# Head attention from one product, and sums, shifted copies and the router moved into other stages

## The reference

```python
x = x + L0_attn_a(ln(x))   # head attention (16 heads of 8, no mask) + state-space scan + gated MLP
x = x + L0_ffn(ln(x))      # two layers: window attention, gated MLP, both on token-shifted input
x = x + L0_attn_b(ln(x))   # head attention, causal
x = x + L0_ffn(ln(x))
x = x + L1_attn_a(ln(x))   # head attention, causal, rotary, with biases
x = x + L1_ffn(ln(x))      # router, top 2 of 8 experts, layer norm of the sum
x = x + L1_attn_b(ln(x))   # random-feature attention
x = x + L1_ffn(ln(x))
```

## Time and profile before

| | |
|---|---|
| median of the runs | 6315.28 us |
| the profiled execution | 6308.24 us |
| its span, first to last instruction | 6306.2 us |
| busy: TensorE, VectorE, ScalarE, GpSimd | 5418.4, 3589.7, 3331.1, 2512.4 us |
| mean granted TensorE clock | 0.948 |

### The profile page before, as it was taken

One profiled execution on the slowest core, in us unless ns is written; L12 is line 12 of the kernel. 1 busy time (PEld: TensorE's weight loads), 2 busy tenths in 40 slices (PEclk: granted clock), 3 DMA queues, 4 the chain that ended last, 5 costly groups with the idle time before them and its releaser, 6 DMA issues. The chain is left out here.

```text
span 6306.2 us, 119595 instructions
## 1 busy us (share of the span) xinstructions
PE 5418.4 (86%) x42357; PEld 2908.8 (46%) x42357; DVE 3589.7 (57%) x4103; ACT 3331.1 (53%) x4993; POOL 2512.4 (40%) x1721
## 2 busy tenths in 40 slices
PE   6876888888887998998898998999897999776998
PEld 2432555555544553564344554554343444343443
DVE  4557999999954554554344554554454343554344
ACT  4555888888854553554444554454343333443343
POOL 1223999999933651652122661662221000000000
PEclk8996999999998999999899999999899999998999
DMA  1002111101011110110000110110000210001121
GB/s 41 1 0 77 31 32 30 33 30 33 29 47 29 40 40 14 41 41 13 1 0 18 45 40 12 42 40 20 28 0 8 54 40 13 0 0 27 32 36 27
DMA packets 136966, 171.03 MB, mean 27 GB/s; under 512 B 32352, under 2 KB 85728, under 8 KB 135520
## 3 DMA queue, kind: packets, MB, share of 16 engines
q1 hardware_dynamic: 136800, 168.85, 10.2%
HBM read 80.11 MB, written 12.85 MB: 15 GB/s over the span
## 5 line engine op out<-in xcount | busy, mean ns | idle before, releaser
L2318 POOL TENSOR_TENSOR arena<-arena,wbig 128x1024 f32<-128x1024 f32 x512 | 1191.8, 2515 | 103.5 <-DMA wbig<-scratch_b 100.3
L2305 DVE TENSOR_TENSOR_SCAN arena<-banks,arena 128x1024 f32<-128x1024 f32 x512 | 1141.5, 2279 | 63.7 <-ACT banks L2249 45.5
L944 ACT ACTIVATE arena<-banks,wbig 128x512 f32<-128x512 f32 x512 | 352.0, 688 | 584.3 <-PE banks L907 572.7
L601 DVE TENSOR_REDUCE arena<-banks 128x4 f32<-128x1024 f32 (+1 forms) x384 | 401.9, 1047 | 432.8 <-PE banks L435 305.1
L957 DVE TENSOR_TENSOR arena<-arena 128x512 f32<-128x512 f32 x512 | 353.3, 692 | 490.2 <-ACT arena L944 434.7
L768 POOL TENSOR_TENSOR X<-X,Z 128x1536 f32<-128x1536 f32 x2 | 9.5, 4758 | 1482.6 <-ACTq L761 1482.6
L1462 POOL TENSOR_TENSOR arena<-arena 128x512 f32<-128x512 f32 x256 | 355.5, 1389 | 594.5 <-DMA arena<-arena 594.5
L2249 ACT ACTIVATE banks<-banks 128x1020 f32<-128x1020 f32 x512 | 518.2, 1012 | 104.3 <-PE banks L2170 96.8
L2254 ACT COPY arena<-banks 128x1024 f32<-128x1024 f32 x512 | 520.8, 1017 | 51.4 <-POOL arena L2318 30.8
L547 ACT ACTIVATE Y<-banks 128x2048 f32<-128x2048 f32 x192 | 305.8, 1593 | 408.4 <-PE banks L471 311.4
L907 PE MATMUL banks<-Z,wbig 128*128 x1024 | 462.2, 597 | 34.3 <-ACTq L56 34.3
(11 more groups left out here) (289 smaller groups left out, 10428.3 us busy)
## 6 DMA issues: line engine op xcount, KB each, us to landing
arena<-arena SPq DMA_DIRECT2D x1024, 64.0 KB, 2.0
arena<-scratch_g SPq DMA_DIRECT2D x32, 1024.0 KB, 13.8
wbig<-scratch_d SPq DMA_DIRECT2D x512, 16.0 KB, 1.7
wbig<-scratch_b SPq DMA_DIRECT2D x64, 128.0 KB, 2.2
wbig<-scratch_c SPq DMA_DIRECT2D x64, 128.0 KB, 2.1
arena<-Z SPq DMA_DIRECT2D x64, 128.0 KB, 2.1
wbig<-in_l_ffn SPq DMA_DIRECT2D x1, 4197.0 KB, 12.9
X<-in_x SPq DMA_DIRECT2D x2, 2048.0 KB, 14.7
```

The lines of the kernel that those rows point to most:

```text
L601: dve.tensor_reduce(to, mbank[:, :, :, 0:keys], AX_X, ALU.max).then_inc(dve_m.sem, 1)
L944: act.activation(hid[e % 2][:, f, :], hbank[f], ACT.Relu, bias=b1[:, e, f:f + 1])\
L2305: dve.tensor_tensor_scan(own, line(decay_bank[n % 2]), own, 0.0, ALU.mult, ALU.add)\
L2318: pool.tensor_tensor(four(h[par][:, m * 1024:m * 1024 + 1024]), four(us[n % 2]), Bs[par].unsqueeze(1).to_broadcast([128, 4, SEQ]), ALU.mult)\
```

## The change

In head attention the eight columns of a head's values are followed by eight columns of ones in the same 32-wide weight, two heads to a product, and the second pair of heads goes to the other 256 columns of the bank. One product gives outputs and sums; the separate sum products go. The sums then lie on other partitions than the outputs: VectorE copies the bank to SBUF, ScalarE takes logarithm and exponential of all 512 columns (output rows become ones), SyncE moves the reciprocals by eight partitions with a DMA, and VectorE multiplies two halves into two tensors, so the output stage takes two products. `qb` and `km` get a second buffer. The value bias is carried through the output matrix into the output bias by a small block.

The shift stages go: GpSimd makes the shifted copies inside the norm, the MLP and the window attention that produce the data. The add stages go: three MLPs and the last norms of the expert blocks write the sum into `X`. Router and experts become one block; the gates are loaded in four quarters, and VectorE waits for a quarter at a time. The core of the diff:

```diff
+def shifted_parts(dst, src, at, width):
+
+    def per_batch(ap, rows):
+        return ap[rows, bass.ds(at, width)].rearrange("p (b t) -> p b t", t=SEQ)
+
+    low, high = slice(0, 64), slice(64, 128)
+    return [(dst[low, bass.ds(at, width)], src[low, bass.ds(at, width)]),
+            (per_batch(dst, high)[:, :, 1:SEQ], per_batch(src, high)[:, :, 0:SEQ - 1])]
...
+                    if add_to is None:
+                        last = dve.tensor_scalar(columns(outs[0][0], t), pre[t % bufs], outs[0][2], None, ALU.add)
+                    else:
+                        last = dve.scalar_tensor_tensor(out=columns(outs[0][0], t), in0=pre[t % bufs],
+                                                        scalar=outs[0][2], in1=columns(add_to, t), op0=ALU.add,
+                                                        op1=ALU.add)
+                    last.then_inc(dve_s.sem, 1)
+
+        if shifted is not None:
+            @block.gpsimd
+            def _(pool):
+                pool.memset(shifted[64:128, 0:TOKENS].rearrange("p (b t) -> p b t", t=SEQ)[:, :, 0:1], 0.0)
+                for t in tiles:
+                    pool.wait_ge(dve_s.sem, dve_s.at(0, f"z{t}"))
+                    for to, own in shifted_parts(shifted, outs[0][0], t * TILE, TILE):
+                        pool.tensor_copy(to, own)
...
-    act_s = Steps(k, "exponentials", ["e0", "ln", "recip", "e1", "shift1", "e2", "e3"], BATCH + 1)
+    act_s = Steps(k, "exponentials", ["e0", "e1", "shift1", "ln", "recip", "e2", "e3"], BATCH + 1)
     act_t = Steps(k, "first_shifts", ["shift0"], BATCH)
     dve_m = Steps(k, "row_maxima", [f"r{n}" for n in range(8)], BATCH)
-    dve_o = Steps(k, "heads_out", ["out"] + (["bias"] if bv is not None else []), BATCH)
+    dve_o = Steps(k, "heads_out", ["raw", "out"], BATCH + 1)
+    moved = Count(k, "reciprocals_moved", 16 * BATCH)
...
-    km = slots(k.arena.take_bf16(4 * SEQ))
-    qb = k.arena.take_bf16(SEQ)
+    km = [slots(k.arena.take_bf16(4 * SEQ)), slots(k.wbig[:, WBIG - 5 * TILE:WBIG - 4 * TILE].bitcast(BF16))]
+    qb = [k.arena.take_bf16(SEQ), k.wbig[:, WBIG - 3 * TILE - SEQ // 2:WBIG - 3 * TILE].bitcast(BF16)]
     shift = slots(k.arena.take_bf16(4 * SEQ))
+    raw, recip, moved_to = (k.wbig[:, WBIG - n * TILE:WBIG - (n - 1) * TILE] for n in (1, 2, 3))
...
-                    pe.wait_ge(dve_o.sem, dve_o.before(i, last_out))
+                    pe.wait_ge(dve_o.sem, dve_o.at(i, "raw"))
                 for u in range(2):
                     j = 2 * jj + u
                     for g in range(4):
-                        pe.matmul(obank[rows(g), first:SEQ], vm[par][:, c, j, rows(g)], prob[s % 2][:, g, u, first:SEQ],
-                                  start=(s == 0 and u == 0), stop=True, skip_group_check=True)
-                    for g in range(4):
-                        last = pe.matmul(obank[rows(g), SEQ + first:2 * SEQ], k.c["slot_ones"][:, rows(j)],
-                                         prob[s % 2][:, g, u, first:SEQ], start=False, stop=True,
+                        last = pe.matmul(obank[rows(g), jj * SEQ + first:(jj + 1) * SEQ], vm[par][:, c, j, rows(g)],
+                                         prob[s % 2][:, g, u, first:SEQ], start=(s == 0 and u == 0), stop=True,
...
+            def logarithm(b):
+                act.wait_ge(dve_o.sem, dve_o.at(b + 1, "raw"))
+                act.wait_ge(dve_o.sem, dve_o.at(b, "out"))
+                act.activation(recip, raw, ACT.Ln, scale=k.c["sum_row"], bias=k.c["head_row"]).then_inc(act_s.sem, 1)
...
                 exponential(i, 0)
+                exponential(i, 1)
+                shifts(i, 1)
                 if back:
+                    logarithm(i - 1)
                     reciprocal(i - 1)
                 else:
                     act_s.skip(act, i, "ln", "recip")
-                exponential(i, 1)
-                shifts(i, 1)
...
+            for par in range(2):
+                for j in range(4):
+                    at = 16 * (j % 2) + HEAD_DIM
+                    last = dve.memset(own_columns(par, j)[:, :, :, at:at + HEAD_DIM], 1.0)
+            last.then_inc(cleared.sem, 1)
             for jj in range(2):
-                last = dve.memset(mx[jj], 0.0)
-            last.then_inc(cleared.sem, 1)
-            dve.wait_ge(cleared.sem, cleared.at(2))
+                dve.memset(mx[jj], 0.0)
+            dve.memset(moved_to, 1.0).then_inc(cleared.sem, 1)
+            dve.wait_ge(cleared.sem, cleared.at(3))
...
+            def heads_raw(b):
+                dve.wait_ge(pe_s.sem, pe_s.at(b + 1, "late"))
+                dve.wait_ge(dve_o.sem, dve_o.at(b, "out"))
+                dve.tensor_copy(raw, obank).then_inc(dve_o.sem, 1)
+
             def heads_out(b):
-                dve.wait_ge(act_s.sem, act_s.at(b + 1, "recip"))
-                to = out[:, bass.ds(b * SEQ, SEQ)]
-                dve.tensor_tensor(to, obank[:, 0:SEQ], recip, ALU.mult).then_inc(dve_o.sem, 1)
-                if bv is not None:
-                    dve.wait_ge(dve_o.sem, dve_o.at(b, "out"))
-                    dve.tensor_scalar(to, to, bv, None, ALU.add).then_inc(dve_o.sem, 1)
-
+                dve.wait_ge(moved.sem, moved.at(b * 16 + 16))
+                for jj in range(2):
+                    part = slice(jj * SEQ, (jj + 1) * SEQ)
+                    last = dve.tensor_tensor(outs[jj][:, bass.ds(b * SEQ, SEQ)], raw[:, part], moved_to[:, part],
+                                             ALU.mult)
+                last.then_inc(dve_o.sem, 1)
+
+            def trip(b, more):
+                if more:
+                    reduce(b + 1, 0)
+                heads_raw(b - 1)
+                if more:
+                    for n in range(1, 8):
+                        reduce(b + 1, n)
+                heads_out(b - 1)
...
+            def trip(b, par, first=False):
+                keys, queries = kk[:, bass.ds(b * SEQ, SEQ)], q[:, bass.ds(b * SEQ, SEQ)]
+                if not first:
+                    pool.wait_ge(pe_m.sem, pe_m.before(b - 1, "m7"))
+                pool.tensor_copy(qb[par], queries).then_inc(pool_s.sem, 1)
+                pool.tensor_tensor(km[par], spread(keys), mask, ALU.mult).then_inc(pool_s.sem, 1)
...
+        @block.sync
+        def _(sp):
+            for b in range(BATCH):
+                sp.wait_ge(act_s.sem, act_s.at(b + 1, "recip"))
+                sp.wait_ge(dve_o.sem, dve_o.at(b, "out"))
+                sp.dma_start(moved_to[0:128 - HEAD_DIM, :], recip[HEAD_DIM:128, :]).then_inc(moved.sem, 16)
...
+def carried_bias_stage(k, name, parts, bias):
+
+    made, done = Count(k, "carried", 1), Count(k, "carried_added", 1)
+    with k.nc.Block() as block:
+        @block.tensor
+        def _(pe):
+            for n, (w, b) in enumerate(parts):
+                last = pe.matmul(k.psum[:, 0, 0:1], w, b, start=(n == 0), stop=(n == len(parts) - 1))
+            last.then_inc(made.sem, 1)
+
+        @block.vector
+        def _(dve):
+            dve.wait_ge(made.sem, made.at(1))
+            dve.tensor_tensor(bias, k.psum[:, 0, 0:1], bias, ALU.add).then_inc(done.sem, 1)
+            dve.wait_ge(done.sem, done.at(1))
...
+                if dst is add_to:
+                    dve_s.skip(dve, i, "both")
+                else:
+                    dve.tensor_tensor(dst[:, tok(i, TILE)], dst[:, tok(i, TILE)], add_to[:, tok(i, TILE)], ALU.add)\
+                        .then_inc(dve_s.sem, 1)
...
+        if shifted is not None:
+            @block.gpsimd
+            def _(pool):
+                for i in range(TILES):
+                    pool.wait_ge(dve_s.sem, dve_s.at(i, "sum"))
+                    for to, own in shifted_parts(shifted, dst, i * TILE, TILE):
+                        pool.tensor_copy(to, own)
...
+def mixture_stage(k, name, z, w, RT, out):
+
+    nc = k.nc
+    kept = Count(k, "gates_kept", 128)
+    lbank = [k.psum[:, 6 + u, :] for u in range(2)]
+    G = k.arena.take(2 * TILE)
...
+                        if first and u == 0 and e == 2:
+                            act.wait_ge(chain.sem, chain.at(16))
+                            act.activation(ex_, diff, ACT.Exp).then_inc(weighed.sem, 1)
...
+                        if e % 2 == 0:
+                            dve.wait_ge(landed[u][e // 2].sem, landed[u][e // 2].at(i))
...
+                    for q in quads:
+                        own = slice(q * 2, q * 2 + 2)
                         sp.dma_start(gate[u][:, own, :], k.scratch["g"][own, at:at + TILE].unsqueeze(0)
-                                     .to_broadcast([128, 4, TILE])).then_inc(spread[u].sem, 16)
+                                     .to_broadcast([128, 2, TILE])).then_inc(landed[u][q].sem, 16)
...
-    RT, G = k.Y, k.arena.take(2 * TILE)
-    at = k.arena.used
-    kept = Count(k, "gates_kept", 128)
-    router_stage(k, f"{name}_router", k.Z, w, G, RT, kept)
-    k.arena.used = at
-    experts_stage(k, f"{name}_experts", k.Z, w, RT, k.H, kept)
```

(34 more changed lines are left out.)

274 lines of the change are left out of this document (122 added, 152 removed).

## The result

The changed kernel takes 6140.7 us, the median of four runs of 6134.6, 6138.5, 6142.9 and 11525 us, of which the last was disturbed; without it the median is 6138.5. The kernel before takes 6313.9 in the same session. The ratio is 0.9723, with a 95% interval of 0.9704 to 0.9742, so it is faster. The profiled execution took 6138.5 us, its span 6136.8, at the same mean granted clock as before, 0.948. Forecast was 6137.

The account below looks back on a forecast made before the run. TensorE was taken as the bound, with VectorE's looks and reductions next. Terms -113 + 16 + 1.5 - 25.6 - 30.5 - 18.5 - 8 = -178.1 took 6308.2 to 6130.1; plus 7.0 for the median, 6137 us, range 6105 to 6170.

Parts of the forecast that it names:

- Periods: Head-attention stages: time per batch falls from 17.59, 17.88 and 18.87 us to 14.73, 15.60 and 15.60.
- 13.68: First head-attention stage: floor in us a batch, eight looks at 1.71 us, held by VectorE's reduction.
- Attention stages: Three head-attention stages, 15 periods each plus costs at start and tail: -113 us together.
- a granted clock near 0.5 inside an attention stage: Attention stages: listed among the signs that would show the prediction wrong.
- Output stages: Three stages behind head attention, two products a tile: +16 us, four pairs of tiles at 1.35 us each stage.
- Experts: Two router and expert blocks: first gating waits for a quarter of the gates, 9.3 us less each, -18.5 together.
- in one block the issue stays: Merged router and experts: gates' issue keeps its time, waiting for the table in DRAM; first gating moves to 4891.4 us.
- Copies and sums: Eight shift stages and five add stages go, their work moved into the producers: -25.6 and -30.5 us.
- TensorE as the bound: Rival, attention stages: all TensorE loses comes back, 12.8 and 14.6 us a batch, total 6078 us; chance 0.10.
- The port: Rival, attention: `heads_out` meets GpSimd's masked product, VectorE held about 1.5 us a batch, 68 us, total 6205; chance 0.10.
- The window attention hides GpSimd's copies: Window attention: copies hidden by GpSimd's 8.87 us wait; rival, 48 us uncovered or the clock, 6185 us, chance 0.13.
- The transfer: Rival, attention: reciprocals land after 6.7 us (8.5 causal), delaying `heads_out`; about 6365 us at a 13 us landing; chance 0.03.

Follow-up runs that it names:

- the narrow looks: The changed kernel with each row maximum taken over the first half of the keys only, which shortens VectorE's reduction: 6102.1 us.
- the run with the tables moved: The changed kernel with its two new constant columns put behind the cosine and sine tables instead of before them: 6139.0 us.
- the part alone: The kernel before with only the shifted copies made by GpSimd inside the producing stages and the five sums made inside their producers: 6249.7 us, ratio 0.9900.
- the three transfers: The changed kernel with the reciprocals' transfer made three times in a row, each after the one before has landed: 6250.3 us.

## Why the prediction was right, step by step

- **The total.** The terms are right in the main, and the closeness of the total is partly luck. The profiled span fell by 169.4 us, not 178.1, so that the profiled execution came out 8.4 us above the 6130.1 worked out for it. The 7.0 added to get from it to a median was not needed: the profiled execution is itself the middle one of 6134.6, 6138.5 and 6142.9. The two errors cancel to 2 to 4 us.
- **Periods.** Causal: right in every step, 0.08 us off in 15.7. First stage: 14.23 for 14.73. Of the terms on top of 13.68, the copy was right (0.31 for 0.25), `heads_out` sticks out by 0.09 and not 0.35, because most of it falls into the time in which VectorE waits for the next look anyway, and what is left for ScalarE's longer row is under 0.2, not 0.45 (one trip, read by its steps; the split was not run apart). The logarithm was even longer than taken, 0.82 us for 0.63, since its scale and bias are columns. ScalarE is near the bound, as the narrow looks show, but not at it. The Trainium skill, "ScalarE: Activation LUTs", "What ACT_TABLE_LOAD costs", gives an activation of N columns 186 + 0.833 N ns, and 93 more for each operand that is such a column. As an estimate that is 799 ns for 512, and the measured 820 agrees.
- **Attention stages.** -115.0 for -113, two misses that cancel: the first stage gained 45.4 for 38.3, the third 40.4 for 45.2. The third's are in the looks ahead of its first trip, which ran at a mean granted clock of 0.54 for 36 us where before they had 0.72; in the run with the tables moved they had 0.72 again and the stage took 277.1 instead of 280.5. The prediction had named a granted clock near 0.5 inside an attention stage as a sign of being wrong; it came at this one place and cost 3.4 us.
- **Output stages.** Mis-sized: +21.7 for +16. The price of the second product was right: both warm, 15.7 against 10.1 and 10.5 us, +5.6 and +5.3 a stage for +5.4. Left out was what TensorE's 7 us of rest before them does to the clock, 1.8 to 2.6 us a stage. The prediction gave back clock where it removed rests and did not charge it where it added them.
- **Experts.** Mis-sized: -14.8 for -18.5. Issue to gating fell from 14.4 to 5.5 us (8.9 for 9.3). The step that failed is "in one block the issue stays": in the first block the router's chain takes 14.9 us instead of 12.7 from block start to its end, since its one exponential now queues behind ScalarE's activations for the first experts (VectorE waits 1.44 us for it, 0.29 before), and its logits ran at a granted clock of 0.65 (4723 to 4726 us) where they had 0.85 (4865 to 4868). The second part is chance: in four of the other runs the second block's logits ran warm and its chain took 13.3 us. The "first 16 products" of the prediction are 16 records of 8 products; nothing hangs on it.
- **Copies and sums.** -64 for -64.1, the clock's 8 with it; the part alone gave -63.3. One norm of four missed the clock in the changed kernel and two in the one with a single key buffer; in eight other runs none did.
- **Rivals.** TensorE as the bound at 12.8 a batch was not met: even with the looks narrowed the period is 13.85, with ScalarE's exponential in between. The port is real, shown by the three transfers, and missed here only by order. The window attention hides GpSimd's copies. The transfer has a wait only at a stage's end; elsewhere it lands 3.1 us after the issue, and from the reciprocal's end to `heads_out` there are 6.5 to 6.8 us in the first stage and 8.5 in the causal ones (6.7 and 8.5 taken).

What stays open is the four us of "all else". A part has a cause that the prediction left out: the norms behind three of the former add stages now start at 1.00 where they had 0.50 or 0.57, as those behind the shift stages do. The third of them, before and after, is 21.6 and 18.8 us long:

```profile
4451.50:4455.50 4.00, 3.80 (x5) 1.76 (x6) 0.00 (x0) 1.89 (x3) 0.00 (x0) 0.50 0.69 277
```

```profile
4342.20:4346.20 4.00, 3.79 (x9) 1.82 (x10) 0.00 (x0) 3.16 (x5) 0.00 (x0) 1.00 0.77 311
```

Against this the state-space scan and the stage ahead of it, which the change does not touch, are 3.6 us longer in the changed kernel, and other runs move them by as much.

## What to carry to other kernels

When an instruction leaves the busiest engine, work out what the next holder of the loop gives, step by step between two rows of the same kind, and look for the third holder too: here 0.4 us below the second. A tail that lets TensorE rest costs twice, once as the rest and once in the clock of the stage behind it (1.8 to 2.6 us here), so fill it with that stage's own tiles (26 us in three places here). And a helper's one small instruction placed behind a stream of another's work is late by that stream: it is the merged block's price.

## What the runs showed of the hardware that I had not expected

- A VectorE product of two SBUF inputs that starts 0.23 us after a GpSimd product takes 2.11 us instead of 0.42 and ends 0.28 us after GpSimd's.
- The same GpSimd product takes 1.09 or 1.27 us (128x512, float32, one input a broadcast table), by two columns of its table's place.
- The granted clock fell to 0.50 around a rest of 2.4 us behind 24 us of unbroken products, within one us after work had begun again; around a rest of 2.1 us in another block it fell 2 us after.
- Two kernels, the same code up to there: a project stage of 71.0 and of 74.7 us, with a granted clock of 1.00 and 0.75 from 72 to 78 us. A stage's difference of 4 us is not a finding until a second run has it.
